# Second layer's last loop: gelu's half projected first, gelu ahead of the exponential, the table splits in mid step, norms one step sooner

## The chip, the core and the metric

The kernel runs on one core of a Trainium2 chip. The metric is the device time of one execution in microseconds (us). The core has five instruction queues that run side by side and wait for each other by semaphores: PE (TensorE, matmuls and transposes), DVE (VectorE), ACT (ScalarE), POOL (GpSimd) and SP, which here only starts DMAs. R and F are the two SBUF tensors of the kernel (operands rounded for the matmul, and plain f32), PS is PSUM, in eight banks of 512 f32 columns.

## The reference

Eight batches of 512 tokens with 256 features go through two layers. The first is a cross-attention block with an MLP. The second does self-attention, cross-attention on a context of 64 tokens with 16 heads, and a gated MLP, each with a norm ahead and a residual behind:

```
x = _attn(_ln(x, g1, b1), _ln(x, g1, b1), Wq1, Wk1, Wv1, Wo1, bo1) + x
x = _attn(_ln(x, g2, b2), context, Wq2, Wk2, Wv2, Wo2, bo2) + x
h = _ln(x, g3, b3) @ Wp + bp
a, gate = jnp.split(h, 2, axis=-1)
x = a * jax.nn.gelu(gate, approximate=False) @ Wf + bf + x
```

The change concerns all but the first of these lines: the cross-attention and the gated MLP of the second layer.

## The kernel before

The kernel computes every f32 product as three matmuls (`mm3`, lines 144 to 146): each operand is split into a rounded part ("hi") and the rest ("lo"). So each operand that comes out of a matmul costs a copy that rounds (ACT or POOL, lines 154 and 157) and a subtraction that gives the rest (DVE line 160, POOL line 163).

The cross-attention is folded into tables that were worked out at the start: per batch a table of keys times the query weight (`g_b`) and one of values times the output weight (`vw_b`). They come back from DRAM as f32 and are split in the loop by `act_keys`/`act_values` and `pool_keys`/`pool_values`, half a table at a time. The text calls this work the products.

The last loop, `loop4`, has 41 steps (i = 0 to 40). Steps 0 and 1 run inside the end of the self-attention's loop. Step i handles a chunk of 128 tokens i (four chunks a batch, i below 32): scores (12 matmuls of 512 columns), largest value, difference, exponential, sum; of chunk i - 1 the multiplication by the reciprocal on POOL (`p_mul`); of chunk i - 2 the transposes in two halves (`turn`, called first and second turn in the text), their split (`turned`) and the output projection (24 matmuls of 256 columns). From step 8 on it also handles two tiles of the MLP, n = 2(i - 8) and n + 1: `up` (12 matmuls of 512 columns, six for the linear half in bank 4 and six for gelu's half in bank 5), gelu on ACT, the gate on DVE (line 1771: linear half plus bias, times gelu), the rounding on POOL (`rounds`), the rest on DVE (`rests`), and `down` (12 matmuls of 256 columns). Behind the last of eight tiles of a batch DVE adds the residual (line 1806).

Layer norms are spread over such steps by the table `norm4`. Kind "x" is the norm ahead of the cross-attention, kind "g" that ahead of the MLP. A norm takes: statistics on DVE at the end of the step before (lines 237, 241, 244), reciprocal root on POOL (line 254), normalisation on DVE in four operations (line 260), eight transposes on PE (line 150), scale and bias on ACT (`ln_affine`), on POOL the add of the next bias to x and the split (`ln_split_pool`). Here norms stand in steps with i % 4 of 1 (x) and 3 (g), the last in step 35; step 29 has none. A step with one is called a norm step, another a plain step; two neighbours are a pair.

The order on each engine is the order in which the generators `pe_attention2`, `act_attention2`, `dve_attention2` and `pool_attention2` write it. In one step of PE: first turn, scores, second turn, `up(n)`, `down(n - 1)`, output, the norm's transposes, `up(n + 1)`, `down(n)`. Waits are counts of the other engines' events; `up4_mm` counts tiles of `up`, `gelu4` and `gate4` what ACT and DVE have done with them.

## Time and profile before

| | us |
|---|---|
| median of three runs | 2486.8 |
| lowest and highest of them | 2478.7, 2491.9 |
| profiled execution | 2477.08 |
| its span in the profile | 2475.3 |

Over the whole span PE is busy 2173.2 us (88%), DVE 1709.2 (69%), ACT 1307.9 (53%), POOL 1295.9 (52%). The mean granted clock of TensorE is 0.967 of full speed.

The time of an execution is the span and some 2 us around it. Busy times are sums over an engine's instructions; an instruction that is held up while it has started counts as busy for as long. "Idle before" is the time in which the engine had nothing running, with what ended it. The loop of the change takes the stretch from about 1868 us to the end.

### The profile page before, as it was taken

How to read it: one execution, taken by the hardware profiler on the slowest of the kernel's cores; microseconds unless marked ns; L12 is line 12 of the kernel's file. 1: busy time of each engine (PE TensorE's matmuls, PEld its weight loads, DVE VectorE, ACT ScalarE, POOL GpSimd, SP SyncE). 2: the span in 40 equal slices, each digit the busy share in tenths (PEclk: the TensorE clock that was granted, in tenths of full speed). 3: DMA queues.
4: the chain of work that ended last, by engine and by line, in shares of the span. 5: the costliest groups of instructions: out<-in, count | busy, mean ns of one | idle time of the engine just before them, and what ended most of it. 6: DMA issues, size and time to landing. Idle time of an engine off the chain costs nothing.

```text
span 2475.3 us, 31247 instructions
## 1 busy us (share of the span) xinstructions
PE 2173.2 (88%) x11628; PEld 1785.9 (72%) x11628; DVE 1709.2 (69%) x2333; ACT 1307.9 (53%) x1936; POOL 1295.9 (52%) x1023
## 2 busy tenths in 40 slices
PE   6868999987799999999999999999995799999998
PEld 4557777876577777777777777777774687887886
DVE  5566666755777777777777777787774677767653
ACT  5345666643566566665656666566653444444421
POOL 2154555443356565555655556555566854555422
PEclk9878999998899999999999999999998899999999
DMA  7500000010000100001000010000103211111000
GB/s 227 190 25 4 20 20 20 9 69 33 18 23 17 31 14 22 22 14 35 14 22 23 14 35 15 22 23 14 33 21 131 90 35 52 52 35 43 9 9 18
DMA packets 87609, 94.28 MB, mean 38 GB/s; under 512 B 29409, under 2 KB 69089, under 8 KB 87457
## 3 DMA queue, kind: packets, MB, share of 16 engines
q1 hardware_dynamic: 87456, 92.27, 11.5%
q8 instruction: 93, 1.52, 0.3%
q14 instruction: 60, 0.48, 0.1%
HBM read 61.30 MB, written 29.62 MB: 37 GB/s over the span
## 4 chain that ended last, share of the span: by engine, by line
PE 40%; DVE 18%; POOL 16%; issue 14%; ACT 12%; DMA 1%; SPq 0%; POOLq 0%; DVEq 0%; ACTq 0%
PE PS L144 11%; PE PS L146 10%; PE PS L145 10%; POOL R L157 7%; DVE R L160 7%; ACT R L154 6%; POOL R L163 4%; PE PS L1216 3%; DVE F L1434 2%; ACT F L154 2%; PE PS L1220 2%; PE PS L1253 2%; POOL F L1513 2%; ACT F L1352 2%; PE PS L150 1%
## 5 line engine op out<-in xcount | busy, mean ns | idle before, releaser
L144 PE MATMUL PS<-R 128*128 128x512 f32 (+1 forms) x2944 | 1037.8, 353 | 179.3 <-DVE R L160 60.0
L145 PE MATMUL PS<-R 128*128 128x512 f32 (+1 forms) x2944 | 1002.1, 340 | 0.0
L146 PE MATMUL PS<-R 128*128 128x512 f32 (+1 forms) x2944 | 1001.8, 340 | 0.0
L144 PEld LDWEIGHTS PS<-R 128*128 128x128 f32 x2944 | 569.4, 193 | 310.5 <-DVE R L160 77.5
L157 POOL TENSOR_SCALAR R<-F 128x1024 fp32r<-128x1024 f32 (+1 forms) x487 | 543.9, 1121 | 433.6 <-DVE F L1771 229.7
L154 ACT ACTIVATE R<-PS 64x512 fp32r<-64x512 f32 (+4 forms) x860 | 460.4, 546 | 370.4 <-PE PS L146 154.5
L160 DVE TENSOR_TENSOR R<-F,R 128x1024 fp32r<-128x1024 f32 (+2 forms) x416 | 556.0, 1341 | 89.1 <-POOL R L157 66.5
L146 PEld LDWEIGHTS PS<-R 128*128 128x128 f32 x2944 | 569.4, 193 | 62.3
L145 PEld LDWEIGHTS PS<-R 128*128 128x128 f32 x2944 | 570.6, 194 | 54.7
L1352 ACT ACTIVATE F<-PS 128x1024 f32<-128x1024 f32 x256 | 263.3, 1028 | 331.2 <-PE PS L1220 206.1
L160 DVE TENSOR_TENSOR R<-PS,R 128x512 fp32r<-128x512 f32 (+3 forms) x348 | 181.8, 543 | 248.0 <-ACT R L154 247.3
L1434 DVE TENSOR_REDUCE F<-PS 128x2 f32<-128x1024 f32 x256 | 303.5, 1216 | 5.7 <-PE PS L1253 5.1
L157 POOL TENSOR_SCALAR R<-R 64x512 fp32r<-64x512 f32 x128 | 83.8, 666 | 400.8 <-ACT R L154 400.7
L163 POOL TENSOR_TENSOR R<-F,R 128x512 fp32r<-128x512 f32 (+2 forms) x150 | 234.3, 1568 | 61.1 <-ACT R L154 42.9
L1408 DVE TENSOR_TENSOR R<-PS,R 64x512 fp32r<-64x512 f32 x128 | 88.0, 688 | 204.1 <-ACT R L154 204.1
L154 ACT ACTIVATE F<-PS 64x512 f32<-64x512 f32 (+3 forms) x280 | 161.6, 598 | 60.4 <-PE PS L146 53.8
L1216 PE MATMUL PS<-R 128*128 128x512 f32 x512 | 174.0, 421 | 14.7 <-ACT F L1352 13.1
L1253 PE MATMUL PS<-R 128*128 128x512 f32 x512 | 162.8, 400 | 15.9 <-DVE R L160 6.8
L1220 PE MATMUL PS<-R 128*128 128x512 f32 x512 | 163.7, 401 | 11.6 <-ACT R L154 11.6
L1771 DVE SCALAR_TENSOR_TENSOR F<-PS,F 128x512 f32<-128x512 f32 x64 | 47.9, 748 | 116.8 <-ACT F L1713 116.8
L1220 PEld LDWEIGHTS PS<-R 128*128 128x128 f32 x512 | 94.8, 190 | 44.4 <-ACT R L154 25.2
L1216 PEld LDWEIGHTS PS<-R 128*128 128x128 f32 x512 | 86.8, 191 | 51.8 <-ACT F L1352 41.8
(85 smaller groups left out, 1940.1 us busy)
## 6 DMA issues: line engine op xcount, KB each, us to landing
F<-sd SPq DMA_DIRECT2D x128, 128.0 KB, 2.9
gd<-F SPq DMA_DIRECT2D x8, 1024.0 KB, 4.2
vd<-F SPq DMA_DIRECT2D x8, 1024.0 KB, 4.5
xs<-F SPq DMA_DIRECT2D x16, 512.0 KB, 2.6
F<-xs SPq DMA_DIRECT2D x16, 512.0 KB, 3.5
R<-gd SPq DMA_DIRECT2D x8, 1024.0 KB, 5.7
R<-vd SPq DMA_DIRECT2D x8, 1024.0 KB, 5.6
F<-in_x SPq DMA_DIRECT2D x8, 512.0 KB, 5.7
```

The lines of the kernel that those rows point to most:

```text
L144: nc.tensor.matmul(o, L[0], Rr[0], start=start, stop=False, skip_group_check=share)
L145: nc.tensor.matmul(o, L[0], Rr[1], start=False, stop=False, skip_group_check=share)
L146: return nc.tensor.matmul(o, L[1], Rr[0], start=False, stop=stop, skip_group_check=share)
L154: return nc.scalar.activation(o, i, ACT.Identity, **k)
L157: return nc.gpsimd.tensor_scalar(o, i, 1.0, 1.0, ALU.mult, ALU.mult)
L160: return nc.vector.tensor_tensor(o, i, f32(hi), ALU.subtract)
L163: return nc.gpsimd.tensor_tensor(o, i, f32(hi), ALU.subtract)
L1216: nc.tensor.matmul(bank(h), ka[i][h][:, kk], qa[i][h], start=True, stop=False)
L1220: m = nc.tensor.matmul(bank(h), kb[i][h][:, kk], qb[i][h], start=False, stop=True)
L1253: m = nc.tensor.matmul(bank(b0 + h), qa[i][h][:, 128 * q:128 * q + 128], ka[i][h], start=True, stop=True)
L1352: nc.scalar.activation(pst3[n % 2], bank(0, 2), ACT.Exp, scale=0.125).then_inc(e3.sem, 1)
L1434: nc.vector.tensor_reduce(M3[:, q, 0:128:64], bank(b0, 2).rearrange("p (a b) -> p a b", a=2), AX.X, ALU.max).then_inc(b3_max.sem, 1)
```

## The change

PE: `up` projects gelu's half first, and each half has an increment of its own (so `up4_mm` counts two for a tile). The second half projected, the linear one, still waits for the previous gate, and gelu's half for the previous gelu.

ACT: in a step, gelu of tile n comes ahead of the exponential, and the products ahead of the norm's scale and bias and of gelu of n + 1.

DVE: the gate of tile n comes ahead of the normalisation. It also waits for the linear half itself.

POOL: the reciprocal root stands ahead of `p_mul`, and the products between `rounds(n)` and the norm's bias add. The wait of the split for `up` is counted in the new unit.

The norms move one step ahead: x to steps with i % 4 of 0, g to those with 2, the first x norms to 2 and 4, the last norm to step 34.

```diff
-        up4_mm, gelu4, gate4 = event("up_mm", NM), event("gelu", NM), event("gate", NM)
+        up4_mm, gelu4, gate4 = event("up_mm", 2 * NM), event("gelu", NM), event("gate", NM)
...
-            kind = "x" if i % 4 == 1 and i > 1 or i == 2 else "g" if i % 4 == 3 and i >= 7 else None
-            b = i // 4 + 1 if kind == "x" else (i - 7) // 4
+            kind = "x" if i % 4 == 0 and i > 0 or i == 2 else "g" if i % 4 == 2 and i >= 6 else None
+            b = i // 4 + 1 if kind == "x" else (i - 6) // 4
...
-                for g in range(2):
+                for g in (1, 0):
                     pe.wait_ge(gelu4 if g else gate4, n - 1)
...
-                m.then_inc(up4_mm.sem, 1)
+                    m.then_inc(up4_mm.sem, 1)
...
             def gelus(n):
                 m_ = n % 8
-                act.wait_ge(up4_mm, n)
+                act.wait_ge(up4_mm, 2 * n)
...
+                if ok(n, NM):
+                    gelus(n)
                 if ok(i, N4):
                     act.wait_ge(sc_sub, i)
                     nc.scalar.activation(E4[i % 3], E4[i % 3], ACT.Exp, scale=0.125).then_inc(e4.sem, 1)
                 for job in weights_at(i):
                     act_weight(job)
-                if ok(n, NM):
-                    gelus(n)
+                for kind, b, half in products_at(i):
+                    (act_keys if kind == "k" else act_values)(b, half)
                 if i in norm4:
                     kind, _, k = norm4[i]
                     ln_affine(k, *((P_G2, P_B2) if kind == "x" else (P_G3, P_B3)), norm_bank(i))
                 if ok(n + 1, NM):
                     gelus(n + 1)
-                for kind, b, half in products_at(i):
-                    (act_keys if kind == "k" else act_values)(b, half)
...
             def gates(n):
                 m_ = n % 8
+                dve.wait_ge(up4_mm, 2 * n + 1)
                 dve.wait_ge(gelu4, n)
...
+                if ok(n, NM):
+                    gates(n)
                 if i in norm4:
                     kind, b, k = norm4[i]
                     ln_scale(k, X4[b % 5], C)
                 if ok(n, NM):
-                    gates(n)
                     rests(n)
...
+                if i in norm4:
+                    ln_pool_rstd(norm4[i][2])
                 if ok(i - 1, N4):
                     pool.wait_ge(rec4, i - 1)
...
-                if i in norm4:
-                    ln_pool_rstd(norm4[i][2])
                 for job in weights_at(i):
                     pool_weight(job)
                 if ok(n, NM):
                     rounds(n)
+                for kind, b, half in products_at(i):
+                    (pool_keys if kind == "k" else pool_values)(b, half)
...
-                        pool.wait_ge(up4_mm, 8 * (b - 2) + 7)
+                        pool.wait_ge(up4_mm, 2 * (8 * (b - 2) + 7) + 1)
                         ln_split_pool(k, ns4[b % 2])
-                for kind, b, half in products_at(i):
-                    (pool_keys if kind == "k" else pool_values)(b, half)
```

On ACT, a norm step before, from the copies of the turned chunk (L154 R<-PS) over exp (L1725), gelu (L1713) and the norm's scale and bias (L154 F<-PS,F) to the product copy (L154 R<-R):

```order
L154 ACTIVATE R<-PS 128x512 x2
L1725 ACT_TABLE_LOAD
L1725 ACTIVATE F<-F 128x1024
L1713 ACT_TABLE_LOAD
L1713 ACTIVATE F<-PS,F 128x512
L154 ACTIVATE F<-PS,F 128x512 x2
L1713 ACTIVATE F<-PS,F 128x512
L154 ACTIVATE R<-R 128x4x256
```

The same on ACT after the change, where exp is L1727:

```order
L154 ACTIVATE R<-PS 128x512 x2
L1713 ACTIVATE F<-PS,F 128x512
L1727 ACT_TABLE_LOAD
L1727 ACTIVATE F<-F 128x1024
L154 ACTIVATE R<-R 128x4x256
L154 ACTIVATE F<-PS,F 128x512 x2
L1713 ACT_TABLE_LOAD
L1713 ACTIVATE F<-PS,F 128x512
```

The first gelu stands ahead of the load for exp, and the load for gelu behind the norm's work; there are two loads in either.

On DVE, a norm step before, from the differences (L1764) over the normalisation (L260), the gate (L1771) and the rest of the MLP's tile to the add of the attention's output (L1812):

```order
L1764 TENSOR_TENSOR F<-PS,F 128x1024
L260 TENSOR_SCALAR F<-F 128x256 x4
L1771 SCALAR_TENSOR_TENSOR F<-PS,F 128x512
L160 TENSOR_TENSOR R<-F,R 128x512
L1812 TENSOR_TENSOR F<-PS,F 128x256
```

The same on DVE after the change, with the gate as L1772 and the add as L1814:

```order
L1764 TENSOR_TENSOR F<-PS,F 128x1024
L1772 SCALAR_TENSOR_TENSOR F<-PS,F 128x512
L260 TENSOR_SCALAR F<-F 128x256 x4
L160 TENSOR_TENSOR R<-F,R 128x512
L1814 TENSOR_TENSOR F<-PS,F 128x256
```

The gate has moved ahead of the four operations of the normalisation.

On POOL, a norm step before: `p_mul` (L1838), reciprocal root (L254), rounding, bias add (L1851), rounding, split (two rows) and product rest (L163 R<-R):

```order
L1838 TENSOR_TENSOR F<-F 128x1024
L254 TENSOR_TENSOR F<-F 128x4
L157 TENSOR_SCALAR R<-F 128x512
L1851 TENSOR_TENSOR F<-F 128x1024
L157 TENSOR_SCALAR R<-F 128x512
L157 TENSOR_SCALAR R<-F 128x1024
L163 TENSOR_TENSOR R<-F,R 128x1024
L163 TENSOR_TENSOR R<-R 128x4x256
```

The same on POOL after the change, with `p_mul` as L1842 and the bias add as L1855:

```order
L254 TENSOR_TENSOR F<-F 128x4
L1842 TENSOR_TENSOR F<-F 128x1024
L157 TENSOR_SCALAR R<-F 128x512
L163 TENSOR_TENSOR R<-R 128x4x256
L1855 TENSOR_TENSOR F<-F 128x1024
L157 TENSOR_SCALAR R<-F 128x512
L157 TENSOR_SCALAR R<-F 128x1024
L163 TENSOR_TENSOR R<-F,R 128x1024
```

The root comes first, and the product rest stands between the first rounding and the bias add instead of at the end.

## Rows read from the trace of the kernel before

**Rows 1.** Table by stretches: window, length; busy us (instructions) by engine; PEclk; DMA.
```profile
1901.70:1968.10 66.40, 50.80 (x289) 44.31 (x290) 41.93 (x72) 27.43 (x43) 54.91 (x37) 0.88 0.42 137
1968.10:2376.60 408.50, 377.15 (x2287) 327.00 (x2286) 283.83 (x416) 185.62 (x213) 205.99 (x139) 1.00 0.10 34
2376.60:2475.30 98.70, 82.87 (x470) 70.44 (x468) 39.71 (x60) 14.87 (x22) 22.64 (x24) 0.98 0.04 17
```

**Rows 2.** PE's waits, 1996 to 2380 us: waited for, total us, times, longest.
```profile
PE PS L144 <- DVE F L1771: 15.3, 11, 1.5
PE PS L1622 <- DVE R L160: 7.1, 10, 1.4
PE PS L144 <- DVE R L160: 6.5, 11, 0.6
```

**Rows 3.** Timeline of ACT, one norm step and the next: start, length, what.
```profile
2165.18 1.06 ACT L1725 ACTIVATE F<-F 128x1024 f32<-128x1024 f32 x1 [2.20 <-DVE F L1764]
2166.26 1.28 ACT L1713 ACT_TABLE_LOAD   x1
2167.56 0.69 ACT L1713 ACTIVATE F<-PS,F 128x512 f32<-128x512 f32 x1
2169.02 1.45 ACT L154 ACTIVATE F<-PS,F 128x512 f32<-128x512 f32 x2 [0.77 <-PE PS L150]
...
2172.73 1.05 ACT L154 ACTIVATE R<-R 128x1024 fp32r<-128x1024 f32 x1
...
2199.61 1.06 ACT L1725 ACTIVATE F<-F 128x1024 f32<-128x1024 f32 x1 [2.20 <-DVE F L1764]
```

**Rows 4.** Timeline of ACT, first copies of steps 30 and 31.
```profile
2345.51 0.60 ACT L154 ACTIVATE R<-PS 128x512 fp32r<-128x512 f32 x1 [1.18 <-PE PS L1622]
...
2360.54 0.60 ACT L154 ACTIVATE R<-PS 128x512 fp32r<-128x512 f32 x1 [1.18 <-PE PS L1622]
```

**Rows 5.** Timeline of PE: a norm's transposes, and the wait ahead of step 36.
```profile
1967.22 1.03 PE L150 MATMUL PS<-F 128*128 128x128 f32 x8
...
2429.43 0.50 PE L144 MATMUL PS<-R 128*128 128x512 f32 x1 [3.91 <-POOL R L163]
```

**Rows 6.** Timeline of DVE, the norm step of rows 3, and the norm's last statistic.
```profile
2160.86 1.20 DVE L1750 TENSOR_REDUCE F<-F 128x16 f32<-128x1024 f32 x1
...
2163.94 1.21 DVE L1764 TENSOR_TENSOR F<-PS,F 128x1024 f32<-128x1024 f32 x1
2165.34 1.39 DVE L260 TENSOR_SCALAR F<-F 128x256 f32<-128x256 f32 x4 [0.19 <-POOL F L254]
2168.28 0.75 DVE L1771 SCALAR_TENSOR_TENSOR F<-PS,F 128x512 f32<-128x512 f32 x1 [1.55 <-ACT F L1713]
2169.78 2.88 DVE L160 TENSOR_TENSOR R<-F,R 128x512 fp32r<-128x512 f32 x1 [0.75 <-POOL R L157]
...
2192.84 1.33 DVE L244 TENSOR_SCALAR F<-F 128x4 f32<-128x4 f32 x1
```

**Rows 7.** Timeline of POOL, the same steps.
```profile
2164.29 1.01 POOL L254 TENSOR_TENSOR F<-F 128x4 f32<-128x4 f32 x1
2169.12 0.62 POOL L157 TENSOR_SCALAR R<-F 128x512 fp32r<-128x512 f32 x1 [3.81 <-DVE F L1771]
2169.71 2.40 POOL L1851 TENSOR_TENSOR F<-F 128x1024 f32<-128x1024 f32 x1
...
2191.75 2.40 POOL L163 TENSOR_TENSOR R<-R 128x1024 fp32r<-128x1024 f32 x1
```

**Rows 8.** Timeline of ACT in the tail: the last gelu.
```profile
2466.19 0.69 ACT L1713 ACTIVATE F<-PS,F 128x512 f32<-128x512 f32 x1 [3.89 <-PE PS L146]
```

**Rows 9.** Timeline of POOL, step 7: the copy of the norm's split.
```profile
1969.83 1.04 POOL L157 TENSOR_SCALAR R<-F 128x1024 fp32r<-128x1024 f32 x1 [1.27 <-ACT F L154]
```

**Rows 10.** Timelines of DVE and POOL at the kernel's start: L260 between POOL's rests.
```profile
9.81 1.34 DVE L260 TENSOR_SCALAR F<-F 128x192 f32<-128x192 f32 x1
9.78 1.25 POOL L163 TENSOR_TENSOR R<-F,R 64x512 fp32r<-64x512 f32 x1 [0.30 <-ACT R L154]
```

## The prediction

> **What bounds the kernel now.** First the table by stretches. Steps 8 to 31 of the second layer's last loop (1968.1 to 2376.6 us) take 408.5 us, with TensorE (PE) busy for 377 and at its full granted clock, while DVE, ACT and POOL are busy for 284, 186 and 206 [rows 1]. PE is the engine to keep fed there. Before them, steps 2 to 7 (66.4 us) are held by POOL, busy 54.9; behind them lies a tail of 98.7 us with the MLP alone.
>
> Then PE's waits in that loop: 15.3 us in 11 waits for the gate (L1771), 7.1 in 10 before the transposes of the probabilities, 6.5 in 11 before the down projection [rows 2]. Together 28.9 us in about 11 pairs of steps, so 2.6 us a pair. A steady pair, from exponential to exponential, is 2199.61 - 2165.18 = 34.43 us [rows 3].
>
> What would a pair be without waits? The last two steps before the end come near it: ACT's first copies of two steps stand 2360.54 - 2345.51 = 15.03 us apart [rows 4]. A step with a norm has eight transposes more, at most 1.03 us [rows 5]. So a pair without waits is 2 x 15.03 + 1.03 = 31.1 us, and 3.3 us are to be had, somewhat more than the waits' 2.6, because the first matmuls behind a wait run apart.
>
> Third, what each wait comes from. (a) Gate: ACT does exp (2165.18 to 2166.24), loads gelu's table (1.28), then gelu from 2167.56 [rows 3]; DVE's gate follows at 2168.28 [rows 6], and the second up projection waits for it. In plain steps the exp is later, and the wait is the 1.3 us a time of rows 2. (b) Down projection: DVE's rest at 2169.78 takes 2.88 us [rows 6] for 512 columns, which the gate's operation does in 0.75: POOL's bias add (2169.71, 2.40 us) runs until 2172.11 [rows 7], and the rest ends 0.55 us behind it. (c) Transposes: DVE's L244, an operation on 4 columns, takes 1.33 us at 2192.84 [rows 6], until POOL's product rest (2191.75, 2.40 us) is over [rows 7]; the rest that frees the bank is queued behind it. So (b) and (c) are one mechanism: these DVE operations and POOL's exclude each other.
>
> The Trainium skill says the same ("SBUF — State Buffer", section "Who interferes with whom"): the pair of ports is an exclusive lock, for a DVE operation with two SBUF inputs or a tensor_scalar in a two-port mode. The trace agrees, with the 2.88 and 1.33 us. It is the base of rival B.
>
> **The change part by part.** I count from PE's first transpose of a step. A step without waits is 120 times a 256-column matmul (a 512 counts twice) and two turns of about 0.43: (15.03 - 0.86) / 120 = 0.118 us each. So: scores to 3.3, second turn to 3.7, first up projection 3.7 to 6.5 (its first half ready at 5.1), down to 7.9, output to 10.8, in a norm step the transposes to 11.8, second up 2.8 more, down 1.4 more. A result is readable some 0.2 later; that is an estimate from ACT's starts behind PE.
>
> 1. *Gelu's half first, with its own increment, and gelu ahead of exp.* Gelu (0.69) [rows 3] starts at 5.3, no longer behind exp; the gate waits only for the other half (6.7) and for DVE's own order. DVE: first turn's rest at 2.0; from sums to the end of the differences 2165.15 - 2160.86 = 4.29 us [rows 6]; in a plain step with the split in its way the sums start at 4.7 (see 3), so differences end at 9.0 and the gate at 9.7. The second up projection starts at 10.8, its first half needs gelu alone, the gate only 1.4 us later. Wait (a) goes, also in plain steps. Table loads: still two a step, after gelu(n) and before gelu(n+1). ACT in a norm step: gelu 5.3 to 6.0, load to 7.3, exp to 8.4, product copy 1.05 to 9.4, affine (1.45) behind the transposes to 13.4, load to 14.7, gelu to 15.4 [rows 3]; PE needs that gate only in the next step, at 5.1. Covered.
> The Trainium skill ("ScalarE: Activation LUTs", section "What ACT_TABLE_LOAD costs") adds 1.38 us of drain to each load, 2.66 in all. The trace doesn't: from the load's start at 2166.26 to gelu at 2167.56 are 1.30 us [rows 3]. By the page exp would start at 8.6 instead of 7.3; PE's sum is the same by both, and only rival B would become less likely.
>
> 2. *Products ahead of the norm, on ACT and POOL.* The split of the tables moves from the end of a step into its middle: POOL 9.4 to 11.9. So L244 at the end of a plain step (16.4) finds POOL idle, and wait (c) goes. New cover for (b): rests(n) in a norm step now stands behind the product, at 12.5, but the down projection wants it at 14.6, because gate and rounding come 1 us or more earlier than that slot needs. In x steps the two residual adds (of the gate's size, so 1.5 us together, to 14.0) also fit before 14.6.
>
> 3. *Norms a step sooner, reciprocal root first in POOL's step.* Same operations, same number. The root (1.01) [rows 7] now stands before p_mul and holds DVE's rest from 2.0 to 2.5: 0.5 us, covered, since the sums have slack. POOL's split of the normalised tile (1.04 [rows 9] and, by the rests of its size [rows 7], 2.40) falls at 0.8 to 4.3 of the next, plain step: rests(n-1) ends at 4.8, second turn's rest at 7.9, and output wants it at 7.9. This edge has no slack; I keep 0.2 us a pair for it. SP is moved past nothing that waits: x is loaded a step or more before its statistics either way.
>
> 4. *DVE: gate ahead of the normalisation.* Gate ends at 8.0, the four L260 operations (1.39) [rows 6] with POOL's rounding (0.62) [rows 7] between them end at about 9.7; the norm's transposes want them at 10.8. No wait, but see B.
>
> Sum for steps 8 to 31: without waits 24 x 15.03 + 11 norms x 1.03 = 372 us, against 408.5: 36.5 us. Less 0.2 to 0.3 a pair for the edge in 3: **33 us**.
>
> Tail: the last norm moves from step 35 to 34, so that PE's wait of 3.91 us for POOL's split [rows 5] has a step's work over it: 4. Each tile of the MLP alone takes 3.89 + 0.69 = 4.58 us from gelu to gelu [rows 8], against 36 x 0.118 = 4.25 for PE: 0.33 x 10 tiles = 3.3; the last gelu runs beside PE: 0.7. Against that, in step 34 gate, rounding and normalisation (0.75 + 0.62 + 1.39) stand before the transposes, with only a down projection (1.4) over them: a new wait of 1.3. Net **7 us**.
>
> Steps 2 to 7: POOL's work is the same. The wait for ACT's affine (1.27 at 1969.83) [rows 9] gets the product over it, and the root fills a gap of 1 us: 0 to 5 us, taken as **3**.
>
> Together 33 + 7 + 3 = 43 us. The profiled execution is 2477.1 us (span 2475.3), so it would become 2434. It is 9.7 us below the median of the three runs shown; against that median, 2486.8, the forecast is **2443 us**.
>
> **Rivals.** *B: the normalisation is overtaken by the product.* L260 can be held: at 9.81 one of its operations took 1.34 us, since a POOL instruction issued at 9.78 had got between two of the four [rows 10]. In the new norm step POOL's product is ready at 9.4, and I have the last of the four starting at 9.3. If POOL is first, it ends at 12.2 instead of 9.7; the transposes wait 1.5 us, in 11 norm steps 16 us. For it: a margin of 0.1 us, and the timing repeats exactly, so that it is all or nothing. Against: both chains start from the same event, the end of the differences. Time 2443 + 16 = 2459.
>
> *C: half of it.* Besides B, the plain step's edge is missed: rounding (n+1) and the split start a little late, rests(n-1) ends at 6.3, the output projection waits 1.5 us, 12 times: another 18 less, 2477. For it: no slack at that place. Against: DVE's rest asks there within 0.1 us of the split's start and may be first, which makes all of it 2 us earlier.
>
> *D, slower.* The port goes wrong three times a pair: B (1.5), C (1.5), and rests(n) in the norm step stands behind product and bias add both (12.0 + 2.4 + 0.6 = 15.0, and the residual behind it 16.5, against 14.6: 0.4 or 1.9, mean 1.15), with some 0.17 for restarting PE at each: 4.65 us a pair, 56 in all against 43 gained. That is 2500. From 3.6 us a pair on the change loses. Against it: waits don't add up so, as a late transpose moves the down projection later too; and between two POOL instructions DVE got in, since its 2.88 us end with the add.
>
> *E: it doesn't do what it says.* The instruction order shows gelu, load, exp in this order and the norms moved; 2 in 100, 2487.
>
> **How the numbers follow.** Forecast (no wait or small ones, 2430 to 2450) 55 in 100; B 24; C or a mixture 13; D 4; E 2; better than 2430 2. Lower end: all 36.5 + 8.3 + 5 = 50 us, and a median that falls as low as the lowest of the three runs (8 us): 2486.8 - 58, 2428. Upper end: B, with half of C: 2468. About 0.5% (12 us) is what a measurement of this kernel can tell from no change. Faster by more than that means below 2474: forecast, B and half of C, 0.87; same 0.09; slower 0.04.
>
> **What would show it.** In the changed profile: pairs of 31.1 to 31.5 us from exp to exp (B: 32.9); waits of L144 for L1772 gone; gelu(n) 2 us ahead of exp; L244 without its 1.2 us of waiting; the four L260 taking 1.4 to 2.0 us (B: over 4); no wait of 3.9 us in the tail, but one of about 1.3 for L260 in step 34. If PE has no waits left and its clock is still full, but a pair is not near 31.1, my count of the plain step is wrong. If PE waits for a rest again, the port's order was other than I have it.

## The result

The changed kernel takes 2428.1 us (median of 4 runs, 2426.4 to 2430.9); the kernel before takes 2485.4 beside it. The ratio is 0.977, 95% interval 0.974 to 0.980: 57 us faster. The forecast was 2443 (2428 to 2468), so the direction is right. The time stands 0.1 us above the lower end of the range, in the class "better than 2430" that the prediction gave 2 in 100: the range held by a hair. The gain is 57 us against 43 foretold. By the two profiles below it is 50.8; the other 6 come of the profiled executions, 8 us below its kernel's median before and 2 below it after.

The table by stretches of the kernel after, cut as for [rows 1] at TensorE's (PE's) first transposes of steps 2, 8 and 32:

```profile
1905.55:1971.99 66.44, 50.15 (x288) 43.59 (x288) 43.13 (x75) 29.61 (x46) 58.16 (x39) 0.90 0.42 137
1971.99:2337.59 365.60, 365.08 (x2285) 327.67 (x2285) 234.03 (x414) 185.90 (x212) 210.22 (x139) 1.00 0.11 38
2337.59:2424.50 86.91, 77.77 (x470) 68.79 (x468) 36.22 (x60) 14.80 (x22) 19.94 (x22) 1.00 0.05 19
```

| us | before | after | gained | foretold |
|---|---|---|---|---|
| start to step 2 (order not changed) | 1901.7 | 1905.55 | -3.85 | 0 |
| steps 2 to 7 | 66.4 | 66.4 | 0 | 3 |
| steps 8 to 31 | 408.5 | 365.6 | 42.9 | 33 |
| tail | 98.7 | 86.9 | 11.8 | 7 |
| span | 2475.3 | 2424.5 | 50.8 | 43 |

In steps 8 to 31 PE is now busy for 365.08 of 365.60 us at its full clock. The same matmuls counted as 377.15 before: the first ones behind a wait are longer and further apart (the one behind the wait in [rows 5] is 0.50 us long, against 0.39 in an unbroken run). So the 42.9 us are 30.8 of idle time and 12.1 of longer matmuls. PE's waits between 1980 and 2340 us, and (behind the dots) the others behind that:

```profile
PE PS L1622 <- DVE R L160: 1.4, 1, 1.4
PE PS L150 <- DVE F L260: 0.3, 1, 0.3
...
PE PS L150 <- DVE F L260: 1.1, 1, 1.1
PE PS L144 <- DVE R L160: 0.8, 1, 0.8
```

Those of [rows 2] are gone but for one of 1.4 us (the first row here, in step 32), and so is the 3.91 us of [rows 5]. The 1.1 us is the new wait of step 34 that the prediction put at 1.3.

One norm step, on ACT, then DVE, then POOL (start, length, what, [idle before]):

```profile
2129.66 0.69 ACT L1713 ACTIVATE F<-PS,F 128x512 f32<-128x512 f32 x1 [0.78 <-PE PS L146]
2130.36 1.28 ACT L1727 ACT_TABLE_LOAD   x1
2131.66 1.07 ACT L1727 ACTIVATE F<-F 128x1024 f32<-128x1024 f32 x1
2132.63 1.04 ACT L154 ACTIVATE R<-R 128x1024 fp32r<-128x1024 f32 x1
...
2125.73 0.17 DVE L244 TENSOR_SCALAR F<-F 128x4 f32<-128x4 f32 x1
...
2131.23 0.74 DVE L1772 SCALAR_TENSOR_TENSOR F<-PS,F 128x512 f32<-128x512 f32 x1
2131.89 1.68 DVE L260 TENSOR_SCALAR F<-F 128x256 f32<-128x256 f32 x4
2133.49 0.68 DVE L160 TENSOR_TENSOR R<-F,R 128x512 fp32r<-128x512 f32 x1
...
2132.06 0.72 POOL L157 TENSOR_SCALAR R<-F 128x512 fp32r<-128x512 f32 x1 [1.56 <-DVE F L1772]
2133.75 2.65 POOL L163 TENSOR_TENSOR R<-R 128x1024 fp32r<-128x1024 f32 x1 [0.97 <-ACT R L154]
```

Gelu stands 2.0 us ahead of exp. L244 takes 0.17 us against 1.33 [rows 6]. The normalisation (L260) takes 1.68, and the product's rest on POOL starts at 2133.75, just behind it: the last of the four L260 starts at 2133.16, and the copy that POOL's rest needs ends at 2133.67 on ACT, 0.5 us later. This is the race of rival B, won by the normalisation in each of the 11 norm steps of the loop (L260 takes 1.67 or 1.68 us in all). DVE's rest, 2.88 us in [rows 6], takes 0.68, because it too goes ahead of the product.

The 1900 us ahead of step 2 vary between profiled executions by up to 15 us even where nothing in them is changed (1900.4 to 1915.3 among the kernels below). So the experiments are compared by stretches first, cut at the same three transposes, and by whole times where those were taken in several rounds.

### The profile page after: what moved, and what is told of

It reads as the page before. It is cut to its first block and busy times, and to the rows that moved or that the text cites. A ratio compares the mean times of both kernels' runs of the same rounds, so it can differ in the third digit from the quotient of the medians.

```text
span 2424.5 us, 31252 instructions
## 1 busy us (share of the span) xinstructions
PE 2158.2 (89%) x11628; PEld 1786.7 (74%) x11628; DVE 1660.9 (69%) x2333; ACT 1310.4 (54%) x1938; POOL 1299.9 (54%) x1023
## 5 line engine op out<-in xcount | busy, mean ns | idle before, releaser
L154 ACT ACTIVATE R<-PS 64x512 fp32r<-64x512 f32 (+4 forms) x860 | 460.5, 546 | 399.3 <-PE PS L146 155.8
L160 DVE TENSOR_TENSOR R<-F,R 128x1024 fp32r<-128x1024 f32 (+2 forms) x416 | 514.8, 1241 | 79.2 <-POOL R L157 56.2
L163 POOL TENSOR_TENSOR R<-F,R 128x512 fp32r<-128x512 f32 (+2 forms) x150 | 238.0, 1592 | 61.8 <-ACT R L154 43.6
L154 ACT ACTIVATE F<-PS 64x512 f32<-64x512 f32 (+3 forms) x280 | 161.5, 598 | 60.4 <-PE PS L146 54.2
L1216 PEld LDWEIGHTS PS<-R 128*128 128x128 f32 x512 | 86.9, 191 | 51.5 <-ACT F L1352 41.6
L150 PE MATMUL PS<-F 128*128 128x128 f32 x592 | 88.3, 286 | 41.0 <-DVE F L1434 25.4
```

What stands on the lines that cost most here:

```text
L154: return nc.scalar.activation(o, i, ACT.Identity, **k)
L160: return nc.vector.tensor_tensor(o, i, f32(hi), ALU.subtract)
L163: return nc.gpsimd.tensor_tensor(o, i, f32(hi), ALU.subtract)
L1216: nc.tensor.matmul(bank(h), ka[i][h][:, kk], qa[i][h], start=True, stop=False)
```

## The experiments

Two theories. **That of the prediction**: PE waits at places (a), (b) and (c) for two reasons, gelu behind exp, and DVE and POOL locking each other out; each edit of the change mends its place, so the gains add. **Rival**: one edit does nearly all of it, and the others are worth something only beside it, or nothing.

| kernel | 2 to 7 | 8 to 31 | tail | time |
|---|---|---|---|---|
| before | 66.4 | 408.5 | 98.7 | 2485.4 |
| after | 66.4 | 365.6 | 86.9 | 2428.1 |
| b_gelu_first | 66.8 | 374.6 | 95.8 | 2449.7 |
| b_norms_sooner | 72.1 | 413.6 | 91.8 | 2486.1 |
| b_bare_var | 65.9 | 401.9 | 98.6 | 2480.5 |
| a_exp_first | 70.4 | 460.3 | 86.9 | 2531.5 |
| a_exp_scale_first | 72.1 | 396.8 | 86.6 | 2464.5 |
| a_norms_late | 67.2 | 374.2 | 96.3 | 2449.8 |
| a_products_early | 68.5 | 375.9 | 86.9 | 2433.6 |
| a_products_end | 73.1 | 366.5 | 87.0 | 2434.4 |
| a_whole_up | 66.5 | 365.7 | 93.0 | 2431.2 |
| a_late_step1 | 70.5 | 365.6 | 86.9 | 2424.4 |
| a_hold_step4 | 69.2 | 365.3 | 86.6 | 2422.3 |
| a_shared_rests | 67.7 | 365.2 | 86.6 | 2424.0 |

(b_ is an edit of the kernel before, a_ one of the kernel after. The kernel before took 2481 to 2484 us beside the others. Times are medians, but those of b_norms_sooner, b_bare_var, a_exp_first, a_exp_scale_first, a_products_early and a_whole_up are single executions.)

### b_gelu_first: the first part alone

Before's kernel with gelu's half projected first, gelu ahead of exp, and a wait of its own for the gate; norms and products as they were.

```diff
-                for g in range(2):
+                for g in (1, 0):
...
+                if ok(n, NM):
+                    gelus(n)
                 if ok(i, N4):
...
-                if ok(n, NM):
-                    gelus(n)
```

> The kernel before with one part of the change alone: gelu's half projected first, an increment for each half, gelu of tile n ahead of exp on ACT. Products, norms, DVE's and POOL's order stay. Theory: the waits for the gate go (15.3 us and restarts) and the tail's tiles take 4.2 us each; the waits for POOL's port before the transposes and before the down projection stay or shrink a little. 20 to 28 us faster than before. Rival (the waits are replaced by those of the port): under 10 us.

Measured: ratio 0.986 (0.983 to 0.989), some 34 us of time; steps 8 to 31 took 33.9 us less. PE's waits between 1985 and 2335 us were these alone:

```profile
PE PS L144 <- POOL R L163: 6.0, 6, 1.1
```

So the first part alone takes the gate's waits away and those of (b) and (c) as well, which I had put down to the port and given to other edits. The port conflicts do not stop: L244 at the end of the plain steps still takes 1.33 us, as in [rows 6]. DVE's work only stands earlier, so that a held operation ends in time. And a wait comes six times that before had once in its loop (0.8 us): PE now comes to the next tile's up projection before POOL has split the normalised tile.

### a_norms_late: all but the norms

The table of the norms as before's, the rest as after's.

```diff
-            kind = "x" if i % 4 == 0 and i > 0 or i == 2 else "g" if i % 4 == 2 and i >= 6 else None
-            b = i // 4 + 1 if kind == "x" else (i - 6) // 4
+            kind = "x" if i % 4 == 1 and i > 1 or i == 2 else "g" if i % 4 == 3 and i >= 7 else None
+            b = i // 4 + 1 if kind == "x" else (i - 7) // 4
```

> The changed kernel with the norms back at steps with i % 4 of 1 and 3 (and 2, 5, 7). Theory: steps 8 to 31 within 2 us, the tail 4 to 6 us longer, as PE waits there again for POOL's split ahead of step 36. Steps 2 to 7 within 2 us. Rival: the loop also grows, by over 5 us.

Measured: ratio 0.987 (0.984 to 0.990). The loop took 8.6 us more than after's and the tail 9.4. Waits in the loop, then in the tail, then two starts on PE's timeline:

```profile
PE PS L144 <- POOL R L163: 7.9, 6, 2.6
...
PE PS L144 <- POOL R L163: 6.0, 2, 3.9
...
1988.91 0.50 PE L144 MATMUL PS<-R 128*128 128x512 f32 x1 [2.65 <-POOL R L163]
...
2411.04 0.80 PE L144 MATMUL PS<-R 128*128 128x512 f32 x1 [3.87 <-POOL R L163]
```

The same six waits as in b_gelu_first. My expectation of no change in the loop fell: with the other waits gone, the split of a norm taken in step 4k+3 comes too late for the tile that begins a step later. By the stretches the earlier norms are worth 18 us here.

### b_norms_sooner: the norms alone

Before's kernel with the diff of the last experiment turned round.

> The kernel before with one part of the change, the norms a step sooner. Theory: in before's loop no wait for POOL's split of a norm is left, since the gate's waits of (a) and (b) lie over it; so the earlier norms alone are worth nothing in steps 8 to 31 (within 3 us of 408.5) and 4 to 9 us in the tail (98.7), where a split was waited for 4.8 us. The 8.6 us that the norms were worth in the loop of the changed kernel are then a thing of the changed loop alone. Rival: the earlier norms are worth 6 to 10 us in steps 8 to 31 of before too. Rival of the other sign: the norm in the wrong step of before, beside the value products at the step's end, costs over 3 us.

Measured: the loop took 5.1 us more than before's (413.6), the tail 6.9 less. That is the rival of the other sign. The waits in the loop now had this one among them, for the down projection's result to be added by DVE:

```profile
PE PS L144 <- DVE F L1771: 12.8, 9, 1.5
PE PS L144 <- DVE F L1806: 7.6, 4, 1.9
```

So the norms' worth has its sign from the other edit: +8.6 us in the loop beside gelu first, -5.1 without it. The tail, where a split was waited for from the beginning, gains either way. The kernel's loop stands on one execution here, but on steps that repeat: its pairs from step 12 on alternate between 35.6 and 34.4 us, against 34.4 in before.

### a_exp_first: the rest without gelu first on ScalarE

```diff
-                if ok(n, NM):
-                    gelus(n)
                 if ok(i, N4):
                     act.wait_ge(sc_sub, i)
...
                     act_weight(job)
+                if ok(n, NM):
+                    gelus(n)
```

> The changed kernel with exp ahead of gelu of tile n again. Theory (the place of gelu on ACT is what matters, and the gate now stands ahead of the normalisation): in a norm step exp ends about 8.2 us after the step's start, table and gelu about 10.2, gate 10.9, normalisation 12.6, so the norm's transposes wait about 1.8 us: steps 8 to 31 grow by 18 to 25 us. Rival (the split of the up projection alone removes the waits): growth under 5 us.

Measured: the loop took 94.7 us more than after's, and the kernel was slower than before by 49 us (2482.5 beside it). Waits in the loop; then a norm step on DVE, POOL and PE:

```profile
PE PS L150 <- DVE F L260: 34.8, 9, 5.6
PE PS L144 <- DVE R L160: 11.3, 8, 1.4
PE PS L144 <- ACT F L1713: 7.1, 9, 0.8
...
2150.14 0.75 DVE L1772 SCALAR_TENSOR_TENSOR F<-PS,F 128x512 f32<-128x512 f32 x1 [3.18 <-issue]
2150.81 3.69 DVE L260 TENSOR_SCALAR F<-F 128x256 f32<-128x256 f32 x4
...
2151.66 2.37 POOL L163 TENSOR_TENSOR R<-R 128x1024 fp32r<-128x1024 f32 x1
...
2154.64 1.94 PE L150 MATMUL PS<-F 128*128 128x128 f32 x8 [3.65 <-DVE F L260]
2156.24 0.78 PE L144 MATMUL PS<-R 128*128 128x512 f32 x1
2156.81 0.63 PE L145 MATMUL PS<-R 128*128 128x512 f32 x1
2157.24 0.63 PE L146 MATMUL PS<-R 128*128 128x512 f32 x1
```

DVE's gate waits 3.18 us for the late gelu (its own name for the cause is "issue"; gelu's result is what is queued for). Behind the gate stand the four L260. POOL's product gets between them, and they take 3.69 us. The transposes wait 3.65 us. And then PE is slow: eight transposes in 1.94 us against 1.03, matmuls of 512 columns 0.43 apart against 0.23. The table by stretches gives the granted clock behind that wait:

```profile
2154.60:2160.20 5.60, 5.56 (x17) 4.74 (x18) 2.03 (x4) 2.13 (x3) 2.72 (x1) 0.50 0.25 97
```

0.50 is the lower of the clock's two levels (1.2 of 2.4 GHz), behind an idle time of 3.65 us; until it PE had run at its full clock (1.00 from 2125.0 to 2150.9). Over the loop the clock was 0.94 and PE busy for 394.91 us against 365.08. So of the 94.7 us, 29.8 are longer matmuls, most of them by the clock: 0.06 of 460.3 us are 28, an estimate. I had priced such waits as idle time alone.

### a_exp_scale_first: the same, with the normalisation back ahead of the gate

a_exp_first, and on DVE:

```diff
-                if ok(n, NM):
-                    gates(n)
                 if i in norm4:
                     kind, b, k = norm4[i]
                     ln_scale(k, X4[b % 5], C)
+                if ok(n, NM):
+                    gates(n)
```

> After's kernel with the exponential ahead of gelu again, as in a_exp_first, and with VectorE's normalisation (L260) put back ahead of the gate, as before had it. Theory: a_exp_first's 94.7 us in steps 8 to 31 come from the gate standing ahead of the normalisation on VectorE. A late gelu holds the gate, this the normalisation, this runs into POOL's product of the attention, and the transposes of the norm wait 3.8 us for it; the split waits likewise. Then the wait of the transposes (L150 for L260) goes from 34.8 us to under 8, and steps 8 to 31 take 385 to 410 us against 460.3, near before's 408.5. Rival: the order of gelu and exponential itself costs it, by the table loads and the later gelu; then steps 8 to 31 stay above 440 us.

Measured: 396.8 us in the loop, inside the expected 385 to 410, and no wait for L260. So 63.5 of the 94.7 us came from the gate standing ahead of the normalisation, and 31.2 are what gelu first is worth here, near the 33.9 that it gave alone. The order on DVE is no part of the 31.2: a_hold_step4 below has this order beside the early gelu, and its loop takes 365.3 us. So the gate ahead of the normalisation gains nothing with gelu early, and costs 63.5 us with gelu late.

### a_products_early: rival B, made on purpose

ACT's copy of the product moved ahead of gelu, so that POOL's rest of it is asked for before the normalisation is through.

```diff
+                for kind, b, half in products_at(i):
+                    (act_keys if kind == "k" else act_values)(b, half)
                 if ok(n, NM):
                     gelus(n)
...
-                for kind, b, half in products_at(i):
-                    (act_keys if kind == "k" else act_values)(b, half)
```

> The changed kernel with ACT's product copy moved ahead of gelu, so that POOL's product is ready right behind its rounding and gets between the four operations of the normalisation: rival B of the prediction, made on purpose. Theory (DVE's tensor_scalar and POOL exclude each other): the four L260 take over 4 us instead of 1.68, the norm's transposes wait 1.0 to 1.8 us, steps 8 to 31 grow by 12 to 19 us. Rival (POOL's instruction doesn't hold DVE): L260 stays at 1.7 us and the stretch within 2 us.

Measured: 10.3 us more in the loop. Waits; then DVE, POOL and PE in a norm step:

```profile
PE PS L150 <- DVE F L260: 4.7, 9, 0.5
...
2166.94 3.75 DVE L260 TENSOR_SCALAR F<-F 128x256 f32<-128x256 f32 x4
...
2167.79 2.42 POOL L163 TENSOR_TENSOR R<-R 128x1024 fp32r<-128x1024 f32 x1
...
2170.83 1.06 PE L150 MATMUL PS<-F 128*128 128x128 f32 x8 [0.52 <-DVE F L260]
```

B's mechanism is real: the four operations take 3.75 us instead of 1.68, as POOL's rest lies between them. The transposes wait 0.52 us here, and not the 1.5 of my sum; a pair took 31.28 us against 30.57, nine times. The other 3.9 of the 10.3 us are the first pair's (34.06 against 30.17): in step 8 the transposes waited 2.57 us (at 1981.55), and the granted clock was 0.51 over the next 3.5 us. Step 30 has a norm but no product, and its L260 took 1.67 us; so B can strike in 10 steps and not in the 11 of my sum. This is not quite B, though. Counted from the step's first transposes (2159.51) POOL's rest started at 8.3 us, a us sooner than after's (2133.75 - 2124.45 = 9.3), and so it also ended sooner. With B's own timing the wait may be up to a us longer, which is an estimate. So my 16 was neither shown nor refuted.

### a_products_end: the second part undone

```diff
-                for kind, b, half in products_at(i):
-                    (act_keys if kind == "k" else act_values)(b, half)
...
                 if ok(n + 1, NM):
                     gelus(n + 1)
+                for kind, b, half in products_at(i):
+                    (act_keys if kind == "k" else act_values)(b, half)
                 yield i
```

and the same on POOL.

> The changed kernel with the products back at the end of the step on ACT and POOL. Theory: L244 is held again in each plain step and the transposes wait 0.5 to 1 us; in norm steps POOL's split comes no later, but the product behind it delays p_mul: steps 8 to 31 grow by 8 to 14 us. Rival (gelu's slack absorbs it, as PE's transposes have slack now too): under 3 us.

Measured: 0.9 us more in the loop, 0.1 in the tail. The rival was right: the order that mends wait (c) is worth nearly nothing there once gelu is early. L244 takes 1.33 us again in nine plain steps, and PE does not wait for it. The 6.7 us more in steps 2 to 7 are another matter. The whole times (2428.9 to 2438.0, ratio 0.980, 0.977 to 0.983) leave room for a few us more than after's, and whether steps 2 to 7 gain by the order is not shown; see a_late_step1.

### b_bare_var: wait (c) by itself

Before's kernel, its last loop's L244 (variance plus epsilon) replaced by a reduction that copies the variance. The 1e-5 is left out there.

```diff
-            nc.vector.tensor_scalar(ve, mv[:, :, 1], EPS, None, ALU.add).then_inc(ln_var.sem, 1)
+            if bare:
+                nc.vector.tensor_reduce(ve, mv[:, :, 1:2], AX.X, ALU.add).then_inc(ln_var.sem, 1)
+            else:
+                nc.vector.tensor_scalar(ve, mv[:, :, 1], EPS, None, ALU.add).then_inc(ln_var.sem, 1)
```

> The kernel before with one instruction replaced: in the last loop, L244 (variance plus 1e-5, a tensor_scalar) becomes a tensor_reduce that copies the variance, so the 1e-5 is left out there. Theory (L244 is held because POOL's product occupies the port, and a reduction with one SBUF input isn't held): it takes about 0.2 us instead of 1.33, PE's wait before the transposes goes (7.1 us in 10 waits, with restarts 8 to 9), steps 8 to 31 shorten by 6 to 9 us. Rival (it is slow for another reason, or the time comes back in the wait for the gate): under 2 us.

Measured: 6.6 us less in the loop, a pair of 33.77 us. DVE's line in place of the 1.33 us of [rows 6]:

```profile
2199.00 0.16 DVE L245 TENSOR_REDUCE F<-F 128x4 f32<-128x4 f32 x1
```

POOL's product rest runs beside it (2197.90, 2.41 us). So (c) was there, and it cost before 6.6 us, although the waits for the gate grew from 16.1 us (12 times) to 19.4 (22 times). It depends on the operation: a reduction of the same 4 columns is not held by POOL. The waits before the down projection, (b), stayed at 6.5 us.

### a_whole_up: what the half-first split does

The linear half first again, and gelu waits for both halves; gelu stays ahead of exp.

```diff
-                for g in (1, 0):
+                for g in range(2):
...
-                act.wait_ge(up4_mm, 2 * n)
+                act.wait_ge(up4_mm, 2 * n + 1)
...
-                dve.wait_ge(up4_mm, 2 * n + 1)
```

> The changed kernel with one part undone: PE projects the linear half first and gelu waits for both halves; all else as changed. Theory (PE is at its own bound in steps 8 to 31, so slack there is not time): steps 8 to 31 stay within 2 us of the changed kernel's 365.5 us, and only the tail grows, from 4.18 us a tile back to about 4.58, 4 to 6 us in all. Rival (the half that gelu needs first is what removes the waits for the gate): steps 8 to 31 grow by 15 us or more and PE waits for the gate's line again.

Measured: 365.7 in the loop, the same, and 6.1 us more in the tail. In the loop it is ACT's order that counts. In the tail, where nothing lies between a tile's up and down projection but the next tile's, the first half counts. Two gelus of the tail, after's and then this kernel's:

```profile
2410.65 0.69 ACT L1713 ACTIVATE F<-PS,F 128x512 f32<-128x512 f32 x1 [3.49 <-PE PS L146]
2414.83 0.69 ACT L1713 ACTIVATE F<-PS,F 128x512 f32<-128x512 f32 x1 [3.49 <-PE PS L146]
```
```profile
2411.14 0.69 ACT L1713 ACTIVATE F<-PS,F 128x512 f32<-128x512 f32 x1 [3.90 <-PE PS L146]
2415.72 0.69 ACT L1713 ACTIVATE F<-PS,F 128x512 f32<-128x512 f32 x1 [3.89 <-PE PS L146]
```

4.18 us a tile against 4.58, the latter as in [rows 8].

### a_late_step1, a_hold_step4, a_shared_rests: steps 1 to 7

After's trace still has a wait of 15.0 us on PE at the end of the self-attention, for POOL's split behind the first product's rests. a_late_step1 puts those rests behind the split:

```diff
                 if i == 2:
+                    for kind, b, half in products_at(1):
+                        (pool_keys if kind == "k" else pool_values)(b, half)
                     after_attention1(pool)
...
-                for kind, b, half in products_at(i):
+                for kind, b, half in (products_at(i) if i != 1 else []):
```

> The changed kernel with one thing more: POOL's three product rests of step 1 (6.9 us) move behind the last work of the self-attention, where POOL then idles for 9 us. PE waits 15.0 us there for POOL's rest. Theory: that wait shrinks by 5 to 7 us and so does the whole time. Rival (the wait is for the reciprocals' way through DRAM, and POOL is only last by name): under 2 us.

Measured: that wait is 8.19 us instead of 15.0. But steps 2 to 7 took 4.1 us more, with this wait in step 4, where after has none:

```profile
1932.33 5.26 DVE L260 TENSOR_SCALAR F<-F 128x256 f32<-128x256 f32 x4 [0.59 <-POOL F L254]
...
1937.65 1.97 PE L150 MATMUL PS<-F 128*128 128x128 f32 x8 [3.87 <-DVE F L260]
```

This is B in step 4: the four L260 against POOL's product of the attention and the weights' rests. In after the same four took 2.04 us. That is no property of the edit. a_exp_first and a_exp_scale_first have the very order of after up to step 7, and there L260 took 5.27 us in step 4 and steps 2 to 7 took 70.4 and 72.1 us against 66.4. So the race in step 4 goes either way in executions of one order.

What sets them apart starts in step 2. Behind the wait for a DMA PE comes back at the clock's lower level, and how long it stays there differs. First and second turn of step 2, in after and (behind the dots) in a_exp_first:

```profile
1905.55 1.08 PE L1622 MATMUL PS<-F 128*128 128x128 f32 x4 [3.61 <-DMA xs<-F]
1910.12 0.60 PE L1622 MATMUL PS<-F 128*128 128x128 f32 x4
...
1912.11 1.09 PE L1622 MATMUL PS<-F 128*128 128x128 f32 x4 [3.62 <-DMA xs<-F]
1918.01 0.60 PE L1622 MATMUL PS<-F 128*128 128x128 f32 x4
```

The granted clock between the two turns was 0.69 in after and 0.51 in a_exp_first, so that the second turn came 4.57 and 5.90 us behind the first. a_whole_up is like after (4.62 us, then 66.5 us for steps 2 to 7); a_exp_scale_first and a_late_step1 are like a_exp_first (6.0 and 5.95 us, then 72.1 and 70.5). In step 4 POOL's L254 then starts 1.97 us ahead of L260 in after and some 1.05 us ahead in those three. The five agree, but that the clock decides the race is argued and not shown by an edit. With one profile of each kernel, differences of up to 6 us in steps 2 to 7 cannot be put down to an edit; those of a_products_end and b_norms_sooner stay open.

a_hold_step4 is a_late_step1 with two things more: POOL waits there, and L260 stands ahead of the gate in all norm steps. The cut shows POOL's part:

```diff
                 if i in norm4:
                     ln_pool_rstd(norm4[i][2])
+                if i == 4:
+                    pool.wait_ge(ln_unit, norm4[i][2])
```

> a_late_step1 (POOL's rests of step 1's product behind the self-attention's last split) with two things more: in step 4 POOL waits, behind the inverse deviation (L254), until VectorE's four normalisations (L260) are done, and goes on with the product only then; and VectorE has L260 ahead of the gate in all norm steps. Theory: L260 takes 1.4 us in step 4 in place of 5.26, since no POOL instruction gets between; PE's wait of 3.9 us goes, POOL loses 1.5 us, and steps 2 to 7 take 66 to 68.5 us against 70.5. In step 34 the wait of 1.1 us for L260 goes and the tail takes 85.8 against 86.9. Steps 8 to 31 stay at 365.6 within 1. Total 2419 to 2423 against 2424.4. Rival: POOL is what steps 2 to 7 go by, and its 1.5 us of hold come back at a later wait for its splits, so that 2 to 7 keep at 69 to 72 us.

Measured: L260 1.37 us in step 4, and no wait of PE for it:

```profile
1928.53 1.37 DVE L260 TENSOR_SCALAR F<-F 128x256 f32<-128x256 f32 x4
...
1929.98 1.91 POOL L1846 TENSOR_TENSOR F<-F 128x1024 f32<-128x1024 f32 x1 [2.42 <-DVE F L260]
```

But POOL stood idle for 2.42 us, PE's waits for its product rose from 1.7 us to 5.3, and steps 2 to 7 took 69.2: nearer to the rival. In this execution the clock was back early in step 2 (second turn 4.59 us behind the first), so the one to compare with is after's, 66.4, and not the 70.5 of a_late_step1: the hold gained nothing there. In step 34 the wait for L260 went, and 0.4 us of waits for a rest took its place; the tail gained 0.3.

a_shared_rests then gives DVE two of three of the weights' rests in steps 2 to 7:

```diff
-        g5 = jobs_of(("p", "f"), w4_stage, 1)
+        g5 = jobs_of(("p", "f"), w4_stage)
...
+                for job in weights_at(i):
+                    dve_weight_rest(job)
```

> a_hold_step4 with two in three of the feed-forward weights' rests in steps 2 to 7 done by VectorE, behind its differences (L1764), in place of all three by POOL. Theory: with the order of the norm in step 4 mended, steps 2 to 7 go by POOL, whose weight rests (3.2 to 3.8 us a step in steps 2 to 4, 2.1 in 5 to 7) stand ahead of the product's and the norm's; two thirds of that, some 10 us in all, go to VectorE, which has 2 to 3.6 us idle in a step. The waits of TensorE for POOL's product of the attention (5.3 us, 4 times) go, and steps 2 to 7 take 62 to 66 us against 69.2; total 2416 to 2420 against 2422.3. Rival: these steps go by the turned transposes, whose copy on ScalarE and rest on VectorE TensorE waits for six times (11.0 us); VectorE's new instructions wait for ScalarE's copies of the weights and hold the next step's rest, and share a port with POOL; then 2 to 7 take 68 to 73 us.

Measured: 67.7 us, between the two, with the clock back early here too (second turn 4.62 us behind the first). The waits for POOL's product fell to 2.4 us, but two rests on DVE took 3.1 to 3.7 us beside POOL in steps 3 and 4, L260 in step 4 came later, and POOL waited 5.08 us for it.

Against before the three have ratios of 0.976 (0.974 to 0.979), 0.977 (0.974 to 0.979) and 0.975 (0.973 to 0.977), the changed kernel 0.977. Their medians are 4 to 6 us below its 2428, and that is not told apart from it.

## Why the prediction was right, and where not

**Direction and place**: right. That the time lies in the range is in part luck: the lower end was made of every term at its best and of a median as low as the lowest run, and the measured time is 0.1 us above it. It read [rows 1] and [rows 2] so that PE is to be fed in steps 8 to 31 and 28.9 us of waits can go there, and they went.

**Term "33 us" for steps 8 to 31, measured 42.9**: mis-sized, in three known pieces. (1) The plain step. It took 15.03 us from [rows 4] as free of waits. The true one is 14.85: in after ACT's first copies stand at 2140.82 and 2155.66 on its timeline, 14.84 apart. The step of [rows 4] had a stop too short for the list of waits, before the second up projection; PE's rows there, of the kernel before, with 0.18 us where 0.12 are usual, and 0.34 where 0.23 are:

```profile
2355.40 0.28 PE L146 MATMUL PS<-R 128*128 128x256 f32 x1
2355.58 0.50 PE L144 MATMUL PS<-R 128*128 128x512 f32 x1
2355.92 0.40 PE L145 MATMUL PS<-R 128*128 128x512 f32 x1
```

24 times 0.18 are 4.3 us. (2) The transposes of a norm took 1.03 by their length, but the next matmul starts 0.79 us behind their start (2165.68 and 2166.47); with the restart it is 0.87 a norm, 15.72 - 14.85. 11 times 0.16 are 1.8 us. (3) The margin for POOL's split in the plain step, 36.5 - 33 = 3.5 us, was not needed. Together 9.6 us of the 9.9 that are missing. A pair measured 30.57 and not 31.1, with no waits and a full clock: that is the prediction's own sign that its count of the plain step was wrong.

**Part 1** (gelu's half first) was right that (a) goes, and too modest. It is worth 33.9 of the 42.9 us with no help from the rest, and 31.2 beside the rest. The half-first split inside it does nothing in the loop and 6.1 us in the tail.

**Part 2** (products in mid step) was given waits (b) and (c). (c) had a real cause at the port (b_bare_var); for (b) the port is argued from [rows 6] and [rows 7], and no run tried it by itself. But b_gelu_first lost both, and a_products_end costs 0.9 us in the loop. Wrong in its attribution: two waits on one path do not sum when one fix gives slack to both.

**Part 3** (norms a step sooner) was costed at nothing or less in the loop, and all of its gain was put in the tail. It is worth 8.6 us in the loop, because the norm in the old step becomes late as soon as gelu first is in. The prediction asked what becomes late when the gate's stall goes, but not for POOL's split of the gate's norm in its old step. The total hid it, since its sum of 372 us without waits took for granted that no new wait would come.

**Part 4** (gate ahead of the normalisation) was foretold to cause no wait, and it causes none. It gains none either: a_hold_step4 undoes it, with 365.3 us in the loop against 365.6 and 0.3 us less in the tail.

**Tail, 7 foretold and 11.8 measured.** The new wait in step 34 was right in place and size (1.1 for 1.3). The tiles were 4.18 us against a foretold 4.25, another 0.7 in ten. The main miss is the wait ahead of step 36: 3.91 us of idle time, but PE ran behind it at the lower clock until 2433.6. Its rows in before, behind the row in [rows 5], and the granted clock of that stretch:

```profile
2430.31 0.63 PE L144 MATMUL PS<-R 128*128 128x512 f32 x1
2430.74 0.63 PE L145 MATMUL PS<-R 128*128 128x512 f32 x1
...
2429.40:2436.00 6.60, 6.44 (x26) 5.26 (x27) 0.75 (x1) 0.69 (x1) 0.38 (x1) 0.74 0.00 0
```

0.26 of 6.6 us are 1.7 more for that wait. Before's tail also had shorter waits that my sum left out: 0.9 us for POOL's split, 0.4 for a rest, and 0.4 for L260, which is part of the 1.1. With the 0.2 of step 34 that is 4.3 of the 4.8 us; the rest stays open.

**Steps 2 to 7, 3 foretold and 0 measured**: that estimate could not have been tested. The stretch varies by up to 6 us in executions of one order. And the unchanged code before it took 3.85 us longer in this execution; the term for it was zero, as it had to be.

**Rivals.** B did not come. Counted from the step's first transposes (2124.45) the product was ready at 9.2 us, near the foretold 9.4, but the last L260 started at 8.7 and not at 9.3: a margin of 0.5 us where the prediction had 0.1. The stake of 24 in 100 followed from a DVE chain counted 0.6 us too late. Made on purpose, a us early, it cost 10 us. The page of the Trainium skill that bears on it ("SBUF — State Buffer", section "Who interferes with whom") calls the shared ports an exclusive lock for such pairs; the 3.75 us of a_products_early agree. C and D did not come. The change's safety hung on one edit: with everything in it but gelu ahead of exp, the kernel was 49 us slower than before.

**Table loads.** In after, exp starts 1.30 us behind the start of its load (2130.36 and 2131.66), as in [rows 3]. The 1.38 us of drain that the Trainium skill adds ("ScalarE: Activation LUTs", section "What ACT_TABLE_LOAD costs") are not there either when gelu stands right ahead of the load. The prediction was right to take the row.

## What to carry to other kernels

When an engine that should never stop waits in several places of a loop, mend the earliest cause first and look again: here one edit gave some three quarters of what the whole change took out of the loop's time (31 to 34 of 43 us), made a second needless in the loop, and gave a third its worth, which alone cost time. Read the granted clock behind each long wait of TensorE (the shortest that cost its clock here was 1.89 us), and price the slower matmuls with the wait. Where a stretch differs between executions of one order, an edit can't be judged in it from one profile. And take the floor of a step from matmul starts, not from a step that merely has no listed wait.

## What the runs showed of the hardware

- **A wait can cost its clock too.** Behind waits of 3.65 and 3.91 us TensorE's granted clock was 0.50 and 0.74 over the next 5.6 and 6.6 us. From step 8 on, in all the kernels here, it fell behind every wait of 3.42 us or more and behind none of up to 1.81 us.
- **In between, the length of the wait alone does not decide.** The clock fell behind 1.89, 2.09, 2.10, 2.15 (twice) and 2.57 us, and stayed full behind 1.87 and 2.65 us (1988.91 in a_norms_late, where the next matmuls of 512 columns came 0.23 apart). In b_norms_sooner two waits of 1.90 us, at 2063.94 and 2133.98, were followed by 0.58 and 1.00 over 4.1 us. There the lower clock did not show in the time: the two pairs of steps took 35.62 and 35.64 us.
- **Four tensor_scalars in a row are not one.** A POOL operation asked for in between is let in: the four L260 take 1.37 us alone, 2.04 to 2.44 with POOL's short work or its last bit beside them, 3.7 with one of 2.4 us between, 5.26 with several. In step 4 it was 2.04 us in one execution and 5.27 in others of the same order, with POOL a us later against DVE.
- **The same 4 columns** take 0.17 us as a tensor_scalar on a free port, up to 2.05 us in after beside POOL (L244 at 1972.96), and 0.16 us as a reduction beside POOL.
- **POOL pays too:** the product's rest took 2.65 us where DVE's rest of 512 columns stood ahead of it, against 2.40 alone [rows 7].
